# A linear-attention recurrence in a transformer block: q kept once, two heads above each other, products in row strips, masked copies last

## What is computed

```python
def step(S, inp):
    rt, kt, vt, wt = inp
    kv = kt[..., :, None] * vt[..., None, :]
    y = jnp.einsum('bhi,bhij->bhj', rt, S + u[None, :, :, None] * kv)
    S = wt[..., None] * S + kv
    return (S, y)
...
yn = ((yh - mu) / jnp.sqrt(var + 0.00064)).reshape(B, T, C) * ln_g + ln_b
return yn * g @ Wo
```

## Time and profile before

| | |
|---|---|
| median of 3 runs | 3821.51 us (3818.33 to 3827.86) |
| span of the profiled execution | 3828.2 us (the page gives no other time of its own for it) |
| busy: TensorE, VectorE, ScalarE, GpSimd | 80%, 64%, 33%, 38% of the span |
| first batch: levels | 399.3 to 442.7 us |
| first batch: y products | 443.7 to 457.3 us |
| first batch: rest of the group norm | 457.3 to 473 us |
| granted TensorE clock, mean | 0.897 |

### The profile page before, as it was taken

How to read it: one execution, slowest core, us unless ns; L and a number is a source line. 1 busy time by engine, 2 the same in 40 slices (tenths; PEclk the granted TensorE clock), 3 DMA queues, 4 the chain that set the end, 5 groups by cost and what they waited for, 6 DMA issues and landing times. The chain is left out here.

```text
span 3828.2 us, 47386 instructions
## 1 busy us (share of the span) xinstructions
PE 3068.0 (80%) x17056; PEld 1877.3 (49%) x17056; DVE 2449.9 (64%) x5133; ACT 1276.0 (33%) x2632; POOL 1463.4 (38%) x1323
## 2 busy tenths in 40 slices
PE   2689767897688975899758997589885898858898
PEld 1235743456434564345633456335573355723557
DVE  5755767547585485854758547585575855768556
ACT  1353033530345312452125521255211542216422
POOL 2224442244513445134551345413454134541344
PEclk9799987999889987899978999789997999969999
DMA  4400023000330003200041000410005000050000
GB/s 129 78 2 1 1 59 64 2 1 1 67 56 2 1 1 78 45 2 1 1 93 30 1 1 1 96 28 2 0 1 109 15 2 0 7 115 2 1 1 12
DMA packets 46763, 106.01 MB, mean 28 GB/s; under 512 B 9713, under 2 KB 30225, under 8 KB 43281
## 3 DMA queue, kind: packets, MB, share of 16 engines
q1 hardware_dynamic: 46480, 102.24, 13.0%
HBM read 65.51 MB, written 35.91 MB: 26 GB/s over the span
## 5 line engine op out<-in xcount | busy, mean ns | idle before, releaser
L803 DVE TENSOR_REDUCE mxp<-PB 128x1 f32<-128x512 f32 (+3 forms) x1536 | 753.2, 549 | 274.7 <-PE PB L1053 182.2
L656 ACT ACTIVATE arena<-PB 128x512 f32<-128x512 f32 (+3 forms) x1536 | 650.5, 509 | 651.3 <-PE PB L1064 646.5
L1050 PE MATMUL PB<-arena 96*128 96x512 bf16 (+3 forms) x1536 | 542.7, 383 | 286.2 <-DMA arena<-parts 214.8
L535 POOL TENSOR_SCALAR_AFFINE_SELECT arena<-arena 128x512 f32<-128x512 f32 x256 | 162.7, 636 | 981.4 <-ACT arena L656 981.0
L1064 PE MATMUL PB<-arena 99*128 99x512 bf16 (+3 forms) x1536 | 467.6, 344 | 16.7 <-DMA arena<-augT 9.5
L1050 PEld LDWEIGHTS PB<-arena 96*128 96x128 bf16 x1536 | 160.8, 106 | 631.6 <-DVE mxp L803 349.2
L1079 PE MATMUL PB<-arena 128*32 128x512 f32 (+3 forms) x3072 | 343.4, 520 | 15.5 <-ACT attn L642 13.7
L1273 PE MATMUL PB<-arena 128*128 128x128 f32 x1792 | 243.4, 293 | 98.3 <-DVE arena L965 98.2
L520 POOL TENSOR_TENSOR hl<-arena,hh 128x512 fp32r<-128x512 f32 x192 | 248.6, 1295 | 192.5 <-ACT hh L673 192.5
L1135 PE MATMUL PB<-xh,wgu 128*128 128x512 f32 x768 | 306.9, 400 | 11.4 <-DVE xres L761 10.8
L1135 PE MATMUL PB<-xl,wgu 128*128 128x512 f32 x768 | 303.3, 395 | 0.0
(11 more groups left out here) (138 smaller groups left out, 5536.3 us busy)
## 6 DMA issues: line engine op xcount, KB each, us to landing
arena<-parts SPq DMA_DIRECT2D x112, 256.0 KB, 10.5
parts<-arena SPq DMA_DIRECT2D x96, 256.0 KB
arena<-parts SPq DMA_DIRECT2D x16, 768.0 KB, 16.0
xres<-in_x SPq DMA_DIRECT2D x16, 512.0 KB, 4.3
arena<-parts SPq DMA_DIRECT2D x16, 512.0 KB, 18.5
out<-xres SPq DMA_DIRECT2D x16, 512.0 KB, 2.9
wlow_dram<-wlow SPq DMA_DIRECT2D x1, 2304.0 KB, 6.8
arena<-augT SPq DMA_DIRECT2D x96, 8.0 KB, 1.8
```

Of the source, the lines that this page charges most:

```text
L656: act.activation(pt[:, U % 3, h, 0:n], bank("score", t)[:, 0:n], ACT.Exp, scale=DH ** -0.5).then_inc(act_emptied, 1)
L803: dve.reduce_max(mxp[:, g % 2, h, col:col + 1], bank("max", g * NPC + k)[:, 0:n], axis=AX.X).then_inc(dve_emptied, 1)
L1050: last = mm(ps[:, 0:n], qst[0:AUG, h, 128 * i:128 * i + 128], kst[0:AUG, h, s0:s0 + n], start=True, stop=not diag)
```

## The change

q is stored once, as `qc`: 128 partitions (two heads of 64 above each other) by 1024 columns for each c. The zeros and their two memsets are gone, and ScalarE copies each bank of r with one instruction. A product of q and one head takes only that head's 64 partitions, so it uses 64 rows of the array, and the two heads' products are issued in turn, each into a bank of its own. So `diag`, `level` and y banks now hold one head of four (or eight) chunks, where they held both heads of half as many. VectorE updates q with one instruction for each level and c, ahead of the two masked copies. The y products are issued chunk by chunk: A v for two heads, q S for two heads. The group norm runs on a bank with four chunks, two halves c and one head, through the views of `gn_views`. The group norm of VectorE and the masked copies of `diag` take their operands by the same pattern. Cut to its core:

```diff
@@ -256,7 +256,7 @@
         gt = take(2048).rearrange("p (i n) -> p i n", i=NT)
-        qd = take(4096).rearrange("p (c h t) -> p c h t", c=NC, h=2)
+        qc = ct(take(2048))
 
@@ -325,6 +324,17 @@
         emptied = {"act": act_emptied, "dve": dve_emptied}
+
+        def gn_views(n):
+
+            q, h = n // 2, n % 2
+
+            def heads(a):
+                return a.rearrange("p i (c h j) -> p i c h j", h=2, j=WH)[:, :, :, h, :]
+
+            i = slice(4 * q, 4 * q + 4)
+            return (heads(xn[:, i, :]), heads(lng[:, 0:1, :].broadcast_to([128, 4, D])),
+                    heads(lng[:, 1:2, :].broadcast_to([128, 4, D])), heads(gt[:, i, :]))
 
@@ -543,10 +553,6 @@
                     ln_scale(2, 1)
-                    pool.memset(qd[0:64, :, 1, :], 0.0).then_inc(qd_zeroed, 1)
-                    pool.wait_ge(qd_zeroed, 1)
-                    pool.memset(qd[64:128, :, 0, :], 0.0).then_inc(qd_zeroed, 1)
-                    pool.wait_ge(qd_zeroed, 2)
                     for n in range(4 * NMIX):
@@ -584,14 +590,13 @@
                         pool.wait_ge(gn_lng, n + 1)
-                        z = xn[:, 2 * n:2 * n + 2, :]
-                        zh = z.rearrange("p i (h j) -> p i h j", j=WH)
-                        r = grs[:, n % 2, :].rearrange("p (i h a) -> p i h a", i=2, a=1).broadcast_to([128, 2, 4, WH])
-                        pool.tensor_tensor(zh, zh, r, ALU.mult).then_inc(gn_chain, 1)
+                        z, gain, shift, gate = gn_views(n)
+                        r = grs[:, n % 2, :].rearrange("p (i c a) -> p i c a", i=4, a=1).broadcast_to([128, 4, NC, WH])
+                        pool.tensor_tensor(z, z, r, ALU.mult).then_inc(gn_chain, 1)
                         pool.wait_ge(gn_chain, 3 * n + 1)
-                        pool.tensor_tensor(z, z, lng[:, 1:2, :].broadcast_to([128, 2, D]), ALU.add).then_inc(gn_chain, 1)
+                        pool.tensor_tensor(z, z, shift, ALU.add).then_inc(gn_chain, 1)
                         pool.wait_ge(gn_chain, 3 * n + 2)
-                        pool.tensor_tensor(z, z, gt[:, 2 * n:2 * n + 2, :], ALU.mult).then_inc(gn_chain, 1)
+                        pool.tensor_tensor(z, z, gate, ALU.mult).then_inc(gn_chain, 1)
                     ln_scale(3, 0)
@@ -706,12 +711,10 @@
                         act.activation(w, w, ACT.Exp, scale=-1.0).then_inc(act_emptied, 1)
-                    act.wait_ge(qd_zeroed, 2)
                     for n in range(4):
                         c, f = n % 2, n // 2
                         wait_filled(act, "r", n)
-                        act.activation(qd[0:64, c, 0, HALF * f:HALF * f + HALF], bank("r", n)[0:64, :], ACT.Copy)
-                        act.activation(qd[64:128, c, 1, HALF * f:HALF * f + HALF], bank("r", n)[64:128, :],
+                        act.activation(qc[:, c, HALF * f:HALF * f + HALF], bank("r", n)[:, :],
                                        ACT.Copy).then_inc(act_emptied, 1)
@@ -947,22 +950,19 @@
                         for c in range(NC):
-                            for q in (0, 1):
-                                n = 4 * l + 2 * c + q
-                                wait_filled(dve, "level", n)
-
-                                dve.wait_ge(dve_emptied, RANK[NTH["level", n - 4] if l else NTH["diag", 7]])
-                                a = A[:, c, 4 * q:4 * q + 4, :, :].rearrange("p n h (b s m) -> p (n h) b s m", s=2, m=m)[:, :, :, 1, :]
+                            n = 4 * l + 2 * c
+                            wait_filled(dve, "level", n + 1)
+                            qv = qc[:, c, :].rearrange("p (n s m) -> p n s m", s=2, m=m)[:, :, 1, :]
+                            w = tm[:, c, :].rearrange("p (n s) -> p n s", s=2)[:, :, 0:1].broadcast_to([128, 512 // m, m])
+                            if l:
+                                dve.wait_ge(q_updated, 2 * (l - 1) + c + 1)
+                            dve.tensor_tensor(qv, qv, w, ALU.mult).then_inc(q_updated, 1)
+                            for h in (0, 1):
+                                dve.wait_ge(dve_emptied, RANK[NTH["level", n + h - 4] if l else NTH["diag", 7]])
+                                a = A[:, c, :, h, :].rearrange("p n (b s m) -> p n b s m", s=2, m=m)[:, :, :, 1, :]
                                 mk = lmask[:, l:l + 1, :].broadcast_to([128, 8, 64]).rearrange("p a (b m) -> p a b m", m=m)
-                                dve.copy_predicated(a, mk, bank("level", n)[:, :].rearrange("p (a b m) -> p a b m", a=8, m=m)
+                                dve.copy_predicated(a, mk, bank("level", n + h)[:, :].rearrange("p (a b m) -> p a b m", a=8, m=m)
                                                     ).then_inc(dve_emptied, 1)
-                            for h in (0, 1):
-                                p = slice(64 * h, 64 * h + 64)
-                                qv = qd[p, c, h, :].rearrange("p (n s m) -> p n s m", s=2, m=m)[:, :, 1, :]
-                                w = tm[p, c, :].rearrange("p (n s) -> p n s", s=2)[:, :, 0:1].broadcast_to([64, 512 // m, m])
-                                if l:
-                                    dve.wait_ge(q_updated, 4 * (l - 1) + 2 * c + h + 1)
-                                dve.tensor_tensor(qv, qv, w, ALU.mult).then_inc(q_updated, 1)
                     dve.wait_ge(s_zeroed, 1)
@@ -1248,31 +1247,36 @@
                     wait_emptied(pe, "r", 3)
-                    for n in range(8):
-                        c, q = n // 4, n % 4
+                    for n in range(0, 8, 2):
+                        c, q = n // 4, n // 2 % 2
                         pe.wait_ge(ku_done, c + 1)
                         wait_bank(pe, "diag", n)
-                        for a in (0, 1):
-                            ch = 2 * q + a
-                            last = mm(bank("diag", n)[:, 256 * a:256 * a + 256].rearrange("p (h t) -> p h t", h=2),
-                                      ku[:, c, 128 * ch:128 * ch + 128], qd[:, c, :, 128 * ch:128 * ch + 128],
-                                      start=True, stop=True)
-                        last.then_inc(filled, 1)
+                        wait_bank(pe, "diag", n + 1)
+                        for a in range(4):
+                            ch = 4 * q + a
+                            for h in (0, 1):
+                                r = slice(64 * h, 64 * h + 64)
+                                last = mm(bank("diag", n + h)[:, 128 * a:128 * a + 128], ku[r, c, 128 * ch:128 * ch + 128],
+                                          qc[r, c, 128 * ch:128 * ch + 128], start=True, stop=True)
+                                if a == 3:
+                                    last.then_inc(filled, 1)
                     for l in range(LEVELS):
                         m = 1 << l
                         for c in range(NC):
-                            for q in (0, 1):
-                                n = 4 * l + 2 * c + q
-                                if l:
-                                    pe.wait_ge(q_updated, 4 * (l - 1) + 2 * c + 2)
-                                    pe.wait_ge(k_updated, 2 * (l - 1) + c + 1)
-                                wait_bank(pe, "level", n)
-                                for a in range(4):
-                                    ch = 4 * q + a
-                                    rhs = qd[:, c, :, 128 * ch:128 * ch + 128].rearrange("p h (b s m) -> p h b s m", s=2, m=m)[:, :, :, 1, :]
-                                    last = mm(bank("level", n)[:, 128 * a:128 * a + 128].rearrange("p (h b m) -> p h b m", h=2, m=m),
-                                              kk[:, c, 128 * ch:128 * ch + 128], rhs, start=True, stop=True)
-                                last.then_inc(filled, 1)
+                            n = 4 * l + 2 * c
+                            if l:
+                                pe.wait_ge(q_updated, 2 * (l - 1) + c + 1)
+                                pe.wait_ge(k_updated, 2 * (l - 1) + c + 1)
+                            wait_bank(pe, "level", n)
+                            wait_bank(pe, "level", n + 1)
+                            for ch in range(NT):
+                                for h in (0, 1):
+                                    r = slice(64 * h, 64 * h + 64)
+                                    rhs = qc[r, c, 128 * ch:128 * ch + 128].rearrange("p (b s m) -> p b s m", s=2, m=m)[:, :, 1, :]
+                                    last = mm(bank("level", n + h)[:, 64 * ch:64 * ch + 64].rearrange("p (b m) -> p b m", m=m),
+                                              kk[r, c, 128 * ch:128 * ch + 128], rhs, start=True, stop=True)
+                                    if ch == NT - 1:
+                                        last.then_inc(filled, 1)
                     for n in range(4):
@@ -1294,19 +1298,25 @@
                     wait_emptied(pe, "level", LEVELS * 4 - 1)
-                    pe.wait_ge(q_updated, 4 * LEVELS)
-                    for n in range(4):
```

(34 more changed lines are left out.)

11 lines of the change are left out of this document (4 added, 7 removed).

## The result

The changed kernel takes 3896.71 us (median of 4 runs, 3890.56 to 3903.22), the kernel before 3824.69 (4 runs): ratio 1.0188, 95% interval 1.0171 to 1.0205. It is 72 us slower, where 74 us less were forecast. 3896.71 lies close to the 3902 of rival (a), but (a)'s mechanism is not what happened.

What follows compares the result with a forecast made beforehand. VectorE was taken to bound the levels, with GpSimd's group norm the next bound. 10.0 + 2.95 - 3.7 = 9.25 us a batch, 74 us for eight batches, gave 3748 us; range 3722 to 3800.

Steps and rivals of the forecast that it cites:

- rival (a): Levels: row strips don't overlap, a TensorE turn takes 3.57 us, the kernel gets slower at 3902 us; chance 10%.
- term 1: Levels: one VectorE update of q replaces two, TensorE's turn takes 2.1 us; 10.0 us a batch gained.
- What costs nothing: ScalarE's r copies, more `diag` products, reordered group norm, q and k updates at once: counted as no cost.
- Rival (b): Levels: strips overlap in part or the clock is low, 2.4 us a turn, 3775 us; chance 13%.
- rule of 2.95: Levels: from a TensorE turn of 2.95 us on, the forecast's sign turns to slower.
- Term 2: GpSimd's two memsets of `qd` go, so VectorE's L753 takes 1.38 us, not 4.33; 2.95 us a batch gained.
- Rival (c): Another wait hides the 2.95 us of the memsets, 3771 us; chance 5%.
- Term 3: y products: bank y0 is read 6.7 us after the first product, with 0.25 us per height change; 3.7 us a batch lost.

Runs made afterwards that it cites:

- full64: The kernel before, each level product split by head at full height, zeros kept, 64 columns, 32 records a turn: 3881.83 us (one run).
- cols2: The changed kernel, with the level products' 64 moving columns streamed twice for seven of the eight chunks: 3758.52 us, ratio 0.9823.
- memset_moved: The kernel before, with its two memsets of qd moved later in GpSimd's program, to where VectorE is idle: 3798.33 us, ratio 0.9934.
- y_grouped: cols2, with each half's y products in two groups, first all A v, then all q S: 3729.19 us, ratio 0.9752.
- cols2y: cols2, with the A v products of y streaming their 64 columns twice as well: 3743.57 us, ratio 0.9787.
- headseq_cols2: The changed kernel, with level products issued head by head and their columns streamed twice: 4023.51 us (one run).
- copies_last: The kernel before, with each half's two q updates moved ahead of its two masked copies in the levels: 3857.62 us, ratio 1.0091.

## Why the prediction was wrong

**The step that failed** is the price of TensorE's turn in term 1. It had two factors. The overlap of row strips was the uncertain one, and it came out a little better than the 1.7 taken: 0.112 (full64) / 0.059 = 1.9. The Trainium skill ("TensorE: Matmul & The Clock Gate", Part 3) has weight loads overlap with running products only where the row group differs; by the runs that agrees in the main (in turn 0.059, head by head 0.092 us a record at the full clock), though head by head lies below the 0.112 of full64 too. The other factor, the granted clock, term 1 took over without a word: its rows, the 0.112 us of the earlier trace rows and the 0.033 us of the earlier trace rows, are from stretches at 1.00. By the runs the clock goes with the products that run and with the waits ahead of them, and both were being replaced. Measured was a turn of 3.41 us at 0.50, for the 2.1 forecast.

**What was put at nothing.** "What costs nothing" has VectorE's copies of `diag` start 3.8 us after the first product, and rival (a) even has the last pair wait for them. That this leaves TensorE idle for 2.21 us just ahead of the levels, and that the clock can fall at it, is not priced. It did in six of eight batches, and their levels are 3.5 us longer than the other two's (47.9 against 44.4 us).

**Rival (b)** named the low clock, with 13%, and priced it by "some turns": 2.4 us a turn, 3775 us. The clock halves nearly all turns, 3.41 us, and that lies beyond the 2.95 from which the sign turns. The rule of 2.95 was right, and I had tied it to (a) alone. A clock of 0.5 over all levels would have been 2 x 1.79 = 3.6 us a turn by my own bounds; it wanted a price and a chance of its own. cols2 shows that the clock is the cause: with the same strips, the same wait in `diag` and more columns it is 1.00 and the time 138 us less. full64 adds that 64 columns at full height, with no such wait ahead, run at 1.00 as well.

**Rival (a)** is refuted, though its 3902 us is within 6 of the result. That is chance: the strips overlap, and 3.41 is near 3.57 because an overlap of nearly two and a clock of a half cancel.

**Term 1 otherwise** holds once the clock is up: 11.9 us a batch in cols2 for 10.0, more even than its bound of 10.6. VectorE's new update takes 0.66 to 0.91 us there, priced at 0.69 to 0.75, and 1.97 only in the first level.

**Term 2** holds: 2.95 us a batch were forecast, 24 us in all, and memset_moved gains 24.8. Rival (c) is out. In the changed kernel the rest of the span is 25 us shorter, which fits, though that rest scatters by up to 21 us.

**Term 3** was right at full clock: 6.7 us to y0 forecast, 6.74 in cols2, where the clock falls only behind y0; 0.25 us a change of height, 0.29 by y_grouped. The Trainium skill ("TensorEngine Tiling (Array Packing)", Key Properties) says that such a change drains the engine; the 0.29 is what this cost here. Wrong was that "y2 and y3 are filled long before its third": with the clock low in half the y stage too, the third round waits 1.44 us, and y costs 5.8 us a batch for 3.7, still 5.2 in cols2, and 4.6 in cols2y, where the clock stays up and nothing waits for y2 and y3.

**The range** of 3722 to 3800 left out what one wrong factor in the engine that decides would do. The lower bound of term 1 in the sum, 8.5 us, has no working, and it holds neither the 3.57 us turn of term 1 nor a low clock. The 0.88 for faster rested on a clock measured on other products.

**Open**: why alternating half-height products of 64 columns don't bring the clock back while TensorE is busy without a gap for 47.9 us, and lose it in two batches after waits of 0.40 and 0.91 us at which cols2 keeps it; and why the clock falls at the same 2.21 us wait in some batches and not in others. The runs show which forms kept or regained it, not the rule. A kernel with the `diag` products of before and the new level products wasn't run, so what the levels would cost without that wait stays open too.

## What to carry to other kernels

When a change replaces the products of a stage that is close to TensorE's bound, price the new ones at both clock levels, and don't carry the granted clock over from the old ones; the sign must survive the lower. Look also at new waits just ahead of the stage: here a clock that fell at one of 2.21 us stayed low for 47.9 us of busy TensorE. And look at the clock of the changed stretch first: if TensorE is full at 0.50, a wasteful form may be the faster one, as here, where streaming the columns twice and grouping the products by height turns 1.9% slower into 2.5% faster than before (y_grouped, the best version found).

## What the hardware showed that was not expected

- TensorE at a granted clock of 0.50 while busy for 30.00 of 30.00 us, in half-height products of 64 columns, after it had run at 1.00 until about 403 us; in six of eight batches the clock had fallen ahead of them, at a wait of 2.21 us, and 47.9 us of back-to-back records did not bring it back. The Trainium skill ("TensorE: Matmul & The Clock Gate", Part 1) describes the slow level as the idle one and the fast one as that of a busy engine; the measurement differs from it here, and it decides.
- Twice the moving columns at no cost: 0.059 us a record with 64 and with 128 columns in alternating strips at the full clock.
- Doubled columns head by head hold 1.00 in three batches and 0.50 in five, each as they found it (headseq_cols2).
- VectorE's updates of q that start together with GpSimd's of k: 2.31 us for two where others take 1.39, 3.92 in the first level (copies_last); in the changed kernel 1.94 for one in the first level, then 0.7, with GpSimd's longer instead (1.66 us for 1.05 to 1.10). What decides which of the two is slowed isn't shown.
